# Turning the first pair of a graph kernel round, with its loads, last roots and last stores in another order

## What is computed

```python
Xw = X @ Wv + bv
e = leaky_relu((Xw @ aw[:d])[:, None, :] + (Xw @ aw[d:])[:, :, None] + ab, 0.2)
alpha = A * exp(e)
transition = alpha / (sum(alpha, -1) + 1e-12)
H, Xk = 0, X
for k in range(3):
    H = H + Xk @ Wk[k] + bk[k]
    Xk = transition @ Xk
x = layernorm(x + relu(H))
x = layernorm(x + (A @ x) @ w)
```

## Time and profile before

| | |
|---|---|
| median of 3 runs | 272.39 us (272.34 to 272.49) |
| the profiled execution | 272.39 us |
| its span, first to last instruction | 270.6 us |
| PE busy | 264.1 us, 98% of the span |
| DVE / ACT / POOL busy | 80% / 71% / 71% |
| DMA engines | 242 to 274 GB/s in the first two of 40 slices, 129 GB/s on average |

### The profile page before, as it was taken

One profiled execution on the slowest core, in us unless ns is written; L12 is line 12 of the kernel. 1 busy time (PEld: TensorE's weight loads), 2 busy tenths in 40 slices (PEclk: granted clock), 3 DMA queues, 4 the chain that ended last, 5 costly groups with the idle time before them and its releaser, 6 DMA issues.

```text
span 270.6 us, 6025 instructions
## 1 busy us (share of the span) xinstructions
PE 264.1 (98%) x1890; PEld 246.1 (91%) x1890; DVE 216.7 (80%) x615; ACT 193.0 (71%) x439; POOL 191.5 (71%) x412
## 2 busy tenths in 40 slices
PE   8899999999999999999999999999999999999992
PEld 5899999999999999999999999999999999999991
DVE  0777798888889888888988888988888898788984
ACT  4887767777666777766777766677776667766874
POOL 4665567778877778887777887777788777657533
PEclk9999999999999999999999999999999999999999
DMA  7997486828955488446873484943884457932214
GB/s 242 274 185 94 85 48 218 131 72 147 168 137 159 81 133 117 155 143 156 140 117 80 154 155 137 152 153 51 131 160 100 118 116 75 125 99 78 80 41 155
DMA packets 28342, 34.91 MB, mean 129 GB/s; under 512 B 6803, under 2 KB 16150, under 8 KB 28310
## 3 DMA queue, kind: packets, MB, share of 16 engines
q1 hardware_dynamic: 27888, 34.12, 60.8%
q10 hardware_dynamic: 422, 0.40, 0.4%
HBM read 26.09 MB, written 8.42 MB: 128 GB/s over the span
## 4 chain that ended last, share of the span: by engine, by line
PE 95%; DMA 2%; DVE 1%; SPq 0%; ACT 0%; issue 0%
PE ps_v L1107 31%; PE ps_y L1107 17%; PE ps_out L1107 15%; PE ps_h L1107 11%; PE ps_agg L1271 10%; PE ps_v L1204 3%; PE ps_v L1208 3%; PE ps_v L1206 3%; DMA WY_sb<-Wk_dram 2%; PE ps_agg L1107 2%; DVE last_out_sb L884 0%; PE ps_v L1254 0%; PE ps_h L1245 0%; PE ps_y L1245 0%; PE ps_agg L1254 0%; DVE WY_lo L669 0%
## 5 line engine op out<-in xcount | busy, mean ns | idle before, releaser
L1107 PE MATMUL ps_v<-WX_hi,XT_hi 128*128 128x512 f32 (+1 forms) x132 | 49.0, 371 | 0.0
L1107 PE MATMUL ps_v<-WX_lo,XT_hi 128*128 128x512 f32 (+1 forms) x132 | 48.6, 368 | 0.0
L1107 PE MATMUL ps_v<-WX_hi,XT_lo 128*128 128x512 f32 (+1 forms) x132 | 48.6, 368 | 0.0
L1029 POOL TENSOR_TENSOR XT_lo<-xt,XT_hi 128x512 fp32r<-128x512 f32 x32 | 42.1, 1319 | 6.6 <-ACT XT_hi L426 6.6
L1039 POOL TENSOR_TENSOR alpha<-exps,adjs 128x256 f32<-128x256 f32 x31 | 23.1, 744 | 28.9 <-ACT exps L470 28.8
L1043 POOL TENSOR_TENSOR alpha_lo<-alpha,alpha_hi 128x256 fp32r<-128x256 f32 x31 | 22.8, 735 | 19.4 <-ACT alpha_hi L479 19.4
L1107 PE MATMUL ps_y<-WY_hi,XT_hi 128*128 128x258 f32 x116 | 35.2, 303 | 0.6 <-DVE WY_lo L673 0.6
L503 ACT ACTIVATE y<-res,offset,rstd 128x256 f32<-128x256 f32 x62 | 33.6, 591 | 2.2 <-POOL offset L1005 2.2
L1271 PEld LDWEIGHTS ps_agg<-adjs,y 128*128 128x128 f32 x248 | 32.0, 191 | 2.2
L1271 PE MATMUL ps_agg<-adjs,y 128*128 128x128 f32 x248 | 32.7, 275 | 0.0
L1107 PE MATMUL ps_y<-WY_lo,XT_hi 128*128 128x258 f32 x116 | 32.7, 282 | 0.0
(11 more groups left out here) (179 smaller groups left out, 830.8 us busy)
## 6 DMA issues: line engine op xcount, KB each, us to landing
xt<-xt_dram SPq DMA_DIRECT2D x32, 256.0 KB, 5.7
nodes<-nodes_dram SPq DMA_DIRECT2D x32, 256.0 KB, 5.8
out_dram<-out_sb SPq DMA_DIRECT2D x30, 256.0 KB, 5.3
adjs<-adjs_dram SPq DMA_DIRECT2D x32, 128.0 KB, 5.7
spread<-si_rows_dram SPq DMA_DIRECT2D x29, 128.0 KB, 4.7
si_rows_dram<-scores SPq DMA_DIRECT2D x29, 1.0 KB, 3.9
WvT_sb<-WvT_dram SPq DMA_DIRECT2D x1, 260.0 KB, 3.6
W_sb<-Wk_dram ACTq DMA_DIRECT2D x1, 256.0 KB, 3.3
```

The lines of the kernel that those rows point to most:

```text
L1029: pool.tensor_tensor(XT_lo[k % 7][:].rearrange("p c b i -> p (c b i)"), xt_sb[k % 4][:], XT_hi[k % 7][:].rearrange("p c b i -> p (c b i)") ...
L1107: last = pe.matmul(to, a, b, start=start and n == 0, stop=stop and n == 2, skip_group_check=True)
```

## The change

1. Loads. WvT goes first on SPq, X of pair 0 follows in two halves, then W1 and X of pair 1. W2 goes first on ACTq, where W0 was; W0 follows the biases there. The weights W0, W1, W2 and w are laid out by partition on the host, so each partition reads one piece of 2 KB in place of two of 1 KB. W2's tile has two spare columns.
2. First pair. PE makes seven warm-up matmuls, score weights, shift, then hop 2 of pair 0 in whole float32 (four matmuls of 258 columns, `first_hop2`), the biases' sum, hop 0, and hop 1. DVE copies u into the whole-float32 W2 tile for it. Hop 2 of pair 1 (`second_hop2`) does all products with the high part of X first. The biases' sum moved to another PSUM place (ps_v).
3. The high part of W0 on ACT moved from second place to behind `v2_hi(3)`, its low part on DVE from the start into `step(0)`. On POOL `xt_lo(0)` stands behind the three small sums for the shift.
4. End. ACT makes the root of graph 0 of pair 31 between the two halves of pair 29's output; DVE takes the reciprocal ahead of the moments of graph 1; SPq stores graph 0 of pair 31 before the half of pair 30.

```diff
@@ sync
-            load_xt(0)
+            half = C * PER * P // 2
             sp.dma_start(WvT_sb[:].rearrange("p c n -> p (c n)"), WvT).then_inc(WvT_loaded, DMA)
-            load_Wk(2)
-            load_Wk(1)
+            sp.dma_start(xt_sb[0][:, 0:half], xt[0, :, 0:half]).then_inc(first_xt_loaded, DMA)
+            sp.dma_start(xt_sb[0][:, half:2 * half], xt[0, :, half:2 * half]).then_inc(xt_loaded[0], DMA)
+            sp.dma_start(W1_sb[:].rearrange("p c n -> p (c n)"), W1).then_inc(Wk_loaded[1], DMA)
             load_xt(1)
-            sp.wait_ge(Wk_loaded[0], DMA)
+            sp.wait_ge(WvT_loaded, DMA)
             load_adjs(0)
...
+            def store_last(b):
+                sp.wait_ge(last_out_ready, b + 1)
+                sp.dma_start(out[LAST, :, b * D:(b + 1) * D], last_out_sb[:, b]).then_inc(last_stored, DMA)
+
+            store_last(0)
             sp.wait_ge(late_half_out_ready, 1)
             sp.dma_start(out[LAST - 1, :, 0:D], out_sb[(LAST - 1) % 3][:, 0]).then_inc(last_stored, DMA)
-            for b in range(PER):
-                sp.wait_ge(last_out_ready, b + 1)
-                sp.dma_start(out[LAST, :, b * D:(b + 1) * D], last_out_sb[:, b]).then_inc(last_stored, DMA)
+            store_last(1)
@@ scalar
-            act.dma_start(W0_sb[:], Wk[0].rearrange("(c p) n -> p c n", p=P)).then_inc(Wk_loaded[0], DMA)
+            act.dma_start(WY_sb[:].rearrange("p c n -> p (c n)"), W2).then_inc(Wk_loaded[2], DMA)
             act.activation(exps[:, 0, 0:1], one, ACT.Exp)
             act.dma_start(bk_sb[:], bk).then_inc(bk_loaded, DMA)
+            act.dma_start(W0_sb[:].rearrange("p c n -> p (c n)"), W0).then_inc(Wk_loaded[0], DMA)
...
+            wy_hi()
+            bk_hi_of()
             xt_hi(0)
-            wx_hi(0)
-            wy_hi()
             wx_hi(1)
-            bk_hi_of()
-            xt_hi(1)
-            xt_hi(2)
             scores_of(0)
             v2_hi(0)
+            xt_hi(1)
             leaky_of(0)
             exponentials(0)
+            xt_hi(2)
+            alpha_hi_of(0)
             xt_hi(3)
-            alpha_hi_of(0)
...
             v2_hi(3)
+            wx_hi(0)
             xt_hi(5)
             xt_hi(6)
@@ vector
+            def score_columns():
+                dve.wait_ge(Wk_loaded[2], DMA)
+                dve.wait_ge(u_done, 1)
+                dve.tensor_copy(WY_sb[:, :, D:D + 2], ps_u).then_inc(u_ready, 1)
+                dve.tensor_copy(WY_hi[:, :, D:D + 2], ps_u).then_inc(u_ready, 1)
...
                 if k == 0:
                     v2_lo(3)
+                    first_hop0_low()
...
+            score_columns()
+            wy_lo()
             bk_lo_of()
             shift_of_scores()
-            first_hop0_low()
+            bias_of_hops()
+            first_hop1_low()
+            v2_lo(0)
             first_hop1(0)
-            v2_lo(0)
             first_alpha()
             first_hop1(1)
             first_alpha_lo()
-            bias_of_hops()
             v2_lo(1)
@@ tensor
+            def first_hop2(c):
+
+                if c == 0:
+                    pe.wait_ge(Wk_loaded[2], DMA)
+                    pe.wait_ge(u_ready, 1)
+                pe.wait_ge(*((first_xt_loaded, DMA) if c == 0 else (xt_loaded[0], DMA)))
+                for b in range(PER):
+                    last = pe.matmul(hop2(0)[:, b, 0:D + 2], first_X[:, c, b], WY_sb[:, c], start=c == 0,
+                                     stop=c == C - 1, skip_group_check=True)
+                if c == C - 1:
+                    last.then_inc(y_done, 1)
...
-            keep_warm(ps_v[:, 0], 8)
+            keep_warm(ps_v[:, 0], 7)
+            score_weights()
+            score_shift()
+            first_hop2(0)
+            first_hop2(1)
+            sum_of_biases()
             first_hop0(0)
-            score_weights()
-            first_hop0(1)
-            score_shift()
-            hop2_and_scores(0)
-            first_hop1(0)
             pe.wait_ge(identity_ready, 1)
             spread_scores(0)
+            first_hop0(1)
+            first_hop1(0)
             first_hop1(1)
-            hop2_and_scores(1)
-            sum_of_biases()
+            second_hop2()
```

More of the change, by code:

```diff
@@ L16, with resnorm_graph_kernel @@
 NORM_EPS = 1e-5
-def resnorm_graph_kernel(nc, xt, adjs, nodes, WvT, Wk, bk, w, si_rows, out):
+def resnorm_graph_kernel(nc, xt, adjs, nodes, WvT, W0, W1, W2, bk, w, si_rows, out):
     PAIRS = nodes.shape[0]
-    D = w.shape[0]
+    D = bk.shape[1]
     C = D // P
-    HOPS = Wk.shape[0]
+    HOPS = bk.shape[0]
     assert (P, C, HOPS) == (nodes.shape[1], 2, 3)
@@ L135, in resnorm_graph_kernel @@
         WvT_loaded = sem("WvT_loaded")
+        first_xt_loaded = sem("first_xt_loaded")
         bk_loaded = sem("bk_loaded")
@@ L981, in _ @@
             last_statistics2(1)
+            last_rstd2_of(0)
             last_mom2(1)
-            for b in range(PER):
-                last_normalise2(b)
+            last_normalise2(0)
+            last_rstd2_of(1)
+            last_normalise2(1)
         @block.gpsimd
@@ L1089, in _ @@
             pool.tensor_tensor(bv_aw_sum[:], bv_aw_chunks[:, 0:1], bv_aw_chunks[:, 1:2], ALU.add).then_inc(bv_aw_ready, 1)
-            for k in range(1, 5):
+            for k in range(5):
                 xt_lo(k)
@@ L1109, in product, with second_hop2 @@
                 return last
+            def first_hop2(c):
[8 more added lines that the diff above has]
+                    last.then_inc(y_done, 1)
+            def second_hop2():
+                pe.wait_ge(WY_ready, 1)
+                pe.wait_ge(shift_ready, 1)
+                pe.wait_ge(xt_hi_ready, 2)
+                for b in range(PER):
+                    for c in range(C):
+                        for n, W in enumerate((WY_hi, WY_lo)):
+                            pe.matmul(hop2(1)[:, b, 0:D + 2], XT_hi[1][:, c, b], W[:, c], start=c == 0 and n == 0,
+                                      stop=False, skip_group_check=True)
+                pe.wait_ge(xt_lo_ready, 2)
+                for b in range(PER):
+                    for c in range(C):
+                        last = pe.matmul(hop2(1)[:, b, 0:D + 2], XT_lo[1][:, c, b], WY_hi[:, c], start=False,
+                                         stop=c == C - 1, skip_group_check=True)
+                last.then_inc(y_done, 1)
             def hop2_and_scores(k, graphs=range(PER)):
-                if k == 0:
-                    pe.wait_ge(WY_ready, 1)
                 pe.wait_ge(xt_lo_ready, k + 1)
[L1117 to L1120, removed]
                 if k > 1:
@@ L1130, in first_hop0 @@
             def first_hop0(b):
-                pe.wait_ge(xt_loaded[0], DMA)
                 pe.wait_ge(Wk_loaded[0], DMA)
-                X = xt_sb[0][:].rearrange("p (c b i) -> p c b i", c=C, b=PER)
                 for c in range(C):
-                    last = pe.matmul(ps_h[:, b], X[:, c, b], W0_sb[:, c], start=b == 0 and c == 0, stop=c == C - 1,
+                    last = pe.matmul(ps_h[:, b], first_X[:, c, b], W0_sb[:, c], start=b == 0 and c == 0, stop=c == C - 1,
                                      skip_group_check=True)
@@ L1404, with by_partition @@
         np.concatenate([WvT, np.concatenate(columns).transpose(2, 1, 0)], axis=2).reshape(P, -1))
-    for name in ("Wk", "bk"):
-        arrays[name] = np.ascontiguousarray(inputs["L0_gnn_" + name])
-    arrays["w"] = np.ascontiguousarray(inputs["L1_gnn_w"])
+    def by_partition(m, room=0):
+        chunks = np.asarray(m).reshape(d // P, P, d).transpose(1, 0, 2)
+        return np.ascontiguousarray(np.pad(chunks, ((0, 0), (0, 0), (0, room))).reshape(P, -1))
+    for hop in range(3):
+        arrays[f"W{hop}"] = by_partition(inputs["L0_gnn_Wk"][hop], 2 if hop == 2 else 0)
+    arrays["bk"] = np.ascontiguousarray(inputs["L0_gnn_bk"])
+    arrays["w"] = by_partition(inputs["L1_gnn_w"])
     nc = bacc.Bacc("TRN2", target_bir_lowering=False, num_devices=1)
```

48 lines of the change are left out of this document (25 added, 23 removed).

## The result

The changed kernel takes 275.66 us in the median of 6 executions (275.38 to 278.92), the kernel before 272.44 in the same session: the ratio is 1.0153 (95% interval 1.0102 to 1.0204), 3.2 us slower by the medians. Two of the six took 278.6 and 278.9. The profiled execution took 275.59 us, 3.20 more than that of before.

A forecast was written before the change was run, and what follows sets the result against it. PE's own work was taken to bound the body, so only entry and way out count: 272.39 - 0.85 (entry) + 0.6 (DVE) - 0.3 (way out) = 271.84, put at 271.8 us, range 271.0 to 272.5.

The forecast's parts named there:

- the rise of the clock: PE's entry: PE leaves the low level, 1.2 GHz, at about 4.6 us; score weights lose 0.3 us to it.
- the gain of the entry: From warm-ups to the start of `propagate_v2(0)`: PE gets there 0.85 us earlier (0.7 to 1.2).
- the length of W0's low part: On DVE in `step(0)`: 0.67 us long, taken from the earlier trace; its insertion delays V1's low part by 0.6.
- third rival: PE's entry: the clock rises only when hop 2 is through, +2.1 us, so 273.9; chance 0.11.
- S: The moment PE starts `propagate_v2(0)`: 13.30 us before, forecast 12.45 with the change.
- the bracket's end of 4.0: First loads: WvT and W2 land between 3.3 and 4.0 us; 3.7 taken, 4.0 makes the sum 0.1 worse.
- the new layout of W2: Loads: pieces of 2 KB in place of 1 KB only help; no size given.
- second rival: The entry gives nothing, through late WvT, late X of pair 4 or ACT; only the end stays, 272.1; chance 0.17.
- the 0.2 from the biases: DVE after S: hop 2 of pair 1 ends later, so V1's low part of pair 0 comes 0.2 us late.
- The rival that DVE does not hold PE up: In `step(0)`: DVE has slack for W0's low part, the 0.6 stays a gain, 271.2; chance 0.20.
- the way out: After the last matmuls: earlier root, reciprocal and stores end the span 0.3 us sooner (0.2 to 0.35).
- X of pair 4: Its load waits for the later hop 0, about 9.5 not 8.0; late by up to 0.4 costs nothing.

The follow-up runs named there:

- thirty thin matmuls: Kernel before with six warm-ups of 512 columns and then thirty matmuls of two columns in place of eight warm-ups: 275.37 us, ratio 1.0117.
- twelve warm-ups: Changed kernel with twelve warm-up matmuls in place of seven, W0's parts still late: 274.46 us, ratio 1.0080.
- W0 late: Kernel before with only W0's two parts made late, inside `propagate_step(0)`, as the change has them: 273.53 us, ratio 1.0049.
- the end alone: Kernel before with only the change's stores, roots and normalisation at the end: 271.94 us, ratio 0.9987.
- hop 2 in its old place: Kernel before with hop 2 of pair 0 in whole float32, order of loads and PE work kept: 272.56 us, ratio 1.0012.
- ten warm-ups: Changed kernel with ten warm-up matmuls in place of seven and both W0 parts made early as in the kernel before: 272.99 us, ratio 1.0033.
- the profile with eight warm-ups: Profiled execution, 278.74 us, of the changed kernel with eight warm-up matmuls in place of seven; median 274.99 us, ratio 1.0066.

## Why the prediction was wrong, step by step

It missed by 3.9 us (271.8, range 271.0 to 272.5), with the wrong sign. Three terms failed: the rise of the clock, the gain of the entry even without that, and the length of W0's low part. Most others hold.

**The step that failed: the rise of the clock stays at 4.6** ("If the rise stays at 4.6, 0.85 us of them run at the low one"). It came at 9.44. The late clock was my third rival, at 0.11. What I set against it, that PE is busy with the score weights up to the rise, does not protect: with thirty thin matmuls PE was as busy and the rise came at 11.18. I also said PE would not wait; it waited 0.42. How much of the delay in the changed kernel is this idle time and how much the score weights, no run separates; with twelve warm-ups ahead of both, the rise came at 4.50.

I also read 4.6 as a fixed moment, from one trace. In four traces with the same rows on PE up to then (eight warm-ups, then hop 0: before, W0 late, the end alone, hop 2 in its old place) the clock rose at 4.62, 3.75, 4.46 and 5.50. Seven warm-ups end at 3.9, so in some executions the rise comes before the gap and in others it would come behind it; whether that is what sorts the executions into groups is not shown.

From warm-ups to S:

| stretch | predicted | measured |
|---|---|---|
| score weights start | 3.76 | 4.32 |
| score weights | 1.14 | 1.73 |
| to hop 2 | 0.4 | 0.52 |
| hop 2 | 1.83 | 3.32 |
| biases to S | 5.35 | 5.37 |
| S | 12.45 | 15.26 |

Of the 2.8 us, 0.56 is WvT (3.7 taken, 4.28 measured, later than the bracket's end of 4.0), 0.6 and 1.5 are the low level. The Trainium skill's rule on shared DMA engines ("DMA: Bandwidth & Descriptors", section "Issuing engines are not separate DMA queues"), which I gave no weight in the sum, was right in kind. The 2.6 us that I took from the earlier trace rows for the lower bound was itself a landing with a load beside it, but with little of it: by the DMA records of the traces, 43 pieces of W0 of 1 KB had been moved when X was in, and in the changed kernel 98 pieces of W2 of 2 KB when WvT was in. Whether the new layout of W2, which I had down as a help, is what does this, no run tests. The third rival priced the low level itself rightly (2.1 us, and 0.6 + 1.5 measured); its 273.9 is too low by WvT's 0.56 and by the 1.0 of W0's low part.

**The gain itself was too large.** With the clock held (ten warm-ups), S is still 13.59 and not 12.45: the start is 0.54 later, the score weights 0.33 shorter, the way to hop 2 0.1 longer, hop 2 with the wait behind it 0.5 longer, since the biases wait for DVE's bk_lo, which lies beside POOL's work (1.49 us for 3 x 256 values, elsewhere 0.41), and the rest 0.3. So the entry gives nothing even then, as the second rival has it; but with W0's dearer part on top the time is 274.46 (twelve warm-ups), outside that rival's 271.9 to 272.5.

**The term that was mis-sized: W0's low part.** "The insertion moves it by 0.6": 1.34 measured alone. The place, the mechanism (no room on DVE, PE waiting at `propagate_v1(1)`) and the 0.2 from the biases (1.61 - 1.34 = 0.27) were right; the duration was not. The earlier trace rows has 0.67 at 8.85 beside POOL too, but there DVE had the ports first: its operations follow one another from 7.79 to 9.52, and it was POOL's pair, begun at 8.48, that took 3.45 us where it takes 2.54. I read the one duration and not what the other engine paid for it. The rival that DVE does not hold PE up is refuted.

**Right:** the way out (0.3 predicted, 0.35 and 0.24 measured), everything behind `propagate_v1(1)`, the biases to S, and X of pair 4, which was issued 12.56 us into the span (before 8.04) with no wait seen for it.

**Open** is what made some executions of several versions take 278: a rise as late as in the profile with eight warm-ups (15.7) would, but I saw it only in that one.

## What to carry to other kernels

Ahead of the rise of TensorE's clock, bridge the wait for the first load with wide matmuls that outlast its latest landing: two too many cost nothing that could be measured in the kernel before, a gap of 1 us or thin matmuls cost 3 us. Don't put work of few columns there. Before an operation is moved to another place on DVE, see what POOL does at that place; with both inputs in SBUF its time is that of the wait for POOL plus its own. And count the first loads as sharing one rate. A moment of the clock read from one trace is one draw: take it from several.

## What the runs showed of the hardware

Thin matmuls of the score weights are halved in speed by the low level like wide ones (1.73 us for eight, 1.57 in the kernel before with six warm-ups, against 0.81), though little of it is columns. The granted clock can fall again after it has risen (1.0 until 7.1, 0.50 until 13.9), with 0.51 us idle and the score weights ahead of it. The column of the granted clock can read 1.00 where the matmuls' spacing is that of the low level, namely ahead of the trace's first entry of the clock (9.44 in the changed kernel); the spacing is what to read. With the same work on PE the first rise came between 3.75 and 5.50 us in four traces. A DVE operation of 128 x 512 with two SBUF inputs ended 0.54 to 0.55 us after the POOL operation that was under way when it began, in seven kernels (1.64 to 1.80 us long), and took 0.69 us where POOL was idle.
